# Expert-key stage: another order of VectorE's work in a tile

## What is computed

```python
q = jnp.einsum('btd,ed->bte', hidden_states, W_q)
q = q.reshape(b, t, 2, h, n).transpose(2, 0, 1, 3, 4)
sim = jnp.einsum('pbthn,hkpn->pbthk', q, keys)              # 4 heads, 2 sides, 64 keys
scores_xy, idx_xy = jax.lax.top_k(sim, K)                   # the 8 best of each side
all_scores = (sx[..., :, None] + sy[..., None, :]).reshape(b, t, h, K * K)
scores, pk = jax.lax.top_k(all_scores, K)                   # the 8 best pairs
w = jax.nn.silu(jnp.einsum('btd,bthkd->bthk', hidden_states, de) * jax.nn.softmax(scores, axis=-1))
experts_states = jnp.einsum('bthk,bthkd->btd', w, ue)
dense = jnp.einsum('bti,di->btd', jax.nn.silu(jnp.einsum('btd,id->bti', hidden_states, W_up)), W_down)
return dense + experts_states
```

## Time and profile before

| | |
|---|---|
| three runs | median 1125.65 us (1123.56 to 1127.57) |
| profiled execution | 1118.98 us, its span 1116.8 us |
| PE busy | 994.8 us (89% of the span) |
| DVE busy | 799.0 us (72%) |
| ACT busy | 652.5 us (58%) |
| POOL busy | 497.9 us (45%) |
| mean granted TensorE clock | 0.963 of full speed |

### The profile page before, as it was taken

The page is one execution under the profiler, slowest core; times in us unless marked ns, Lnnn a source line. Parts: engine busy times, 40 slices in busy tenths (PEclk is TensorE's granted clock), DMA queues, the critical chain, the costliest instruction groups (busy, mean ns, idle before and its releaser), DMA issues.

```text
span 1116.8 us, 17009 instructions
## 1 busy us (share of the span) xinstructions
PE 994.8 (89%) x5550; PEld 632.4 (57%) x5550; DVE 799.0 (72%) x1755; ACT 652.5 (58%) x874; POOL 497.9 (45%) x550
## 2 busy tenths in 40 slices
PE   8889999989778989989999788899998887999991
PEld 3345344434457878778877563344443333888881
DVE  7767688887889798798987446788888844444443
ACT  4357667666566866777777524576675650455550
POOL 6558897896415435335434422215061634222220
PEclk9899999999999999999999989999999988999996
DMA  7855979648999500000003231465644247222226
GB/s 247 239 167 159 291 206 346 196 153 270 235 224 221 117 1 1 0 2 1 1 29 79 75 65 57 123 209 142 172 133 129 83 149 284 61 69 74 70 59 225
DMA packets 74200, 149.87 MB, mean 134 GB/s; under 512 B 7823, under 2 KB 44577, under 8 KB 72580
## 3 DMA queue, kind: packets, MB, share of 16 engines
q1 hardware_dynamic: 61380, 98.80, 33.8%
q0 software_dynamic: 10800, 47.63, 12.0%
q10 hardware_dynamic: 1936, 2.36, 0.6%
HBM read 73.14 MB, written 76.25 MB: 134 GB/s over the span
## 4 chain that ended last, share of the span: by engine, by line
PE 63%; DVE 16%; ACT 9%; issue 4%; POOL 4%; DMA 3%; SPq 1%; ACTq 0%; DVEq 0%; POOLq 0%
PE ps L1318 16%; PE ps L1452 10%; PE ps L1433 7%; PE ps L1418 5%; PE ps L1392 4%; PE ps L1402 4%; PE ps L1660 3%; PE ps L1637 3%; ACT pt L1105 3%; PE ps L1623 3%; DVE negmax L1859 2%; PE ps L1461 2%; PE ps L1783 1%; DVE moe_w L2205 1%; PE ps L1336 1%
## 5 line engine op out<-in xcount | busy, mean ns | idle before, releaser
L1859 DVE TENSOR_REDUCE negmax<-ps 128x2 f32<-128x1024 f32 x256 | 309.6, 1222 | 56.6 <-PE ps L1418 54.1
L1105 ACT ACTIVATE pt<-ps 128x1024 f32<-128x1024 f32 x256 | 259.2, 1027 | 136.1 <-PE ps L1433 134.5
L1452 PE MATMUL ps<-pt,v_aug 128*32 128x512 f32 x1024 | 143.1, 621 | 4.5 <-POOL pt L804 3.6
L1433 PE MATMUL ps<-sq,sk 57*128 57x512 f32 (+1 forms) x512 | 127.5, 496 | 6.0 <-DMA sq<-m_sb 3.5
L1418 PE MATMUL ps<-sk,sq 56*128 56x512 f32 (+1 forms) x512 | 107.8, 424 | 21.2 <-ACT pt L1105 16.1
L804 POOL TENSOR_TENSOR pt<-pt,near 128x256 f32<-128x256 f32 x128 | 92.4, 730 | 49.1 <-ACT pt L1105 48.4
L1433 PEld LDWEIGHTS ps<-sq,sk 57*128 57x128 f32 (+1 forms) x512 | 48.5, 186 | 105.7 <-issue 70.7
L996 POOL DMA_INDIRECT expert_out<-yo,dest x39 | 38.1, 976 | 117.4 <-ACT yo L1285 102.6
L908 POOL TENSOR_TENSOR w_first<-w_first,moe_w 128x1024 f32<-128x1024 f32 x16 | 38.1, 2383 | 106.4 <-DVE pt L2197 105.7
L1623 PE MATMUL ps<-sel,hl 128*128 128x512 f32 x256 | 73.4, 422 | 13.3 <-DVE pt L2197 13.3
L1418 PEld LDWEIGHTS ps<-sk,sq 56*128 56x128 f32 (+1 forms) x512 | 49.4, 190 | 42.4 <-ACT pt L1105 27.9
(11 more groups left out here) (323 smaller groups left out, 2083.6 us busy)
## 6 DMA issues: line engine op xcount, KB each, us to landing
expert_rows<-zero SPq DMA_DIRECT2D x3, 5586.0 KB, 61.4
expert_weights_split<-wst POOLq DMA_DIRECT2D x8, 2048.0 KB, 8.7
qk_rows<-hl SPq DMA_DIRECT2D x30, 512.0 KB, 3.1
sk<-qk_rows SPq DMA_DIRECT2D x62, 192.0 KB, 5.1
sq<-qk_rows SPq DMA_DIRECT2D x62, 192.0 KB, 4.5
moe_w<-in_w POOLq DMA_DIRECT2D x16, 512.0 KB, 7.7
wexp<-expert_weights_split POOLq DMA_DIRECT2D x16, 512.0 KB, 4.9
wexp<-expert_weights_split SPq DMA_DIRECT2D x4, 2048.0 KB, 16.4
```

The source lines that it names most:

```text
L1105: act.activation(pt[:, 4 * (U % 2) + 2 * half:4 * (U % 2) + 2 * half + 2, :], ps[:, bank:bank + 2, :], ACT.Exp, scale=(BIAS, SCALE)[L]).th ...
L1433: ins = pe.matmul(ps[:, key.bank + s, :], sk[r, pair, c * P:(c + 1) * P], sq[r, pair, :], start=True, stop=True)
L1452: ins = pe.matmul(ps[32 * j:32 * j + 32, OBANK, :], v_aug[:, b % 2, c, HG * g + j, :], pt[:, 4 * (U % 2) + j, :], start=(c == 0), stop=(c ...
L1859: dve.tensor_reduce(negmax[:, n % 2, col:col + 9:8], ps[:, job.bank:job.bank + 2, :], AX, ALU.max, negate=True).then_inc(s_jd, 1)
```

## The change

Only the order of VectorE's stream changes; no instruction is added or removed on any engine. `top8(n)` is cut into `side_top8(n)` (with the wait for `s_cl` at its head) and `pair_top8(n)`. In the loop, `side_top8(s + 1)` moves ahead of `turned_low(s)`; `norm1` moves from the middle of odd steps to the step before, ahead of `mask(s, 0)` (and stays in step 1, ahead of its first mask); `norms8(s)` moves behind `times_hidden(s, 3)`; `pair_rest` moves from the middle of an odd step to the end of the even step ahead of it (in step 15 the last one stays where it was).

```diff
--- before.py
+++ after.py
@@ -1999,6 +1999,10 @@
                     dve.tensor_scalar(xnb_first[p][:, t % 2, :], x_tok[:, 0, t, :], mv1[:, t, 0:1], rstd1[:, t:t + 1], ALU.subtract, ALU.mult).then_inc(s_n1, 1)
 
             def top8(n):
+                side_top8(n)
+                pair_top8(n)
+
+            def side_top8(n):
                 r = n % RING
                 if n >= 2:
                     dve.wait_ge(s_cl, n - 1)
@@ -2011,6 +2015,10 @@
                 own(dve.tensor_tensor(s64[:, n % 2], sxy[:, r, :, 0, :].unsqueeze(3).broadcast_to([P, RH, 8, 8]),
                                       sxy[:, r, :, 1, :].unsqueeze(2).broadcast_to([P, RH, 8, 8]), ALU.add))
                 own(dve.tensor_reduce(mag[:], sxy[:, r].rearrange("p h s j -> p h (s j)"), AX, ALU.add, apply_absolute_value=True))
+
+            def pair_top8(n):
+                r = n % RING
+                sim = simcat[n % 2].rearrange("p (h s k) -> p h s k", h=RH, s=2)
                 for h in range(RH):
                     own(dve.max_index(ix8[:, h, :], sxy[:, r, h, 0, :], sim[:, h, 1]))
                 own.wait()
@@ -2262,9 +2270,10 @@
                     dve.tensor_scalar(xnb[:, t % 2, :], x_tok[:, 0, t, :], mv[:, 0, t, 0:1], rstd[:, 0, t:t + 1], ALU.subtract, ALU.mult).then_inc(s_cn, 1)
 
             for s in range(NTL):
+                if 2 <= s + 1 < NTL:
+                    side_top8(s + 1)
                 if s >= 2:
                     turned_low(s)
-                odd_norm = s % 2 and (s + 3) // 2 < NTL // 2
                 if s % 2 and s >= 5:
                     pair_sum((s - 5) // 2)
                 if s == 3:
@@ -2275,7 +2284,9 @@
                 if s in (10, 13):
                     rstd2_seed(s // 13, s // 13 + 1)
                 if 2 <= s + 1 < NTL:
-                    top8(s + 1)
+                    pair_top8(s + 1)
+                if s == 1 or s >= 2 and s % 2 == 0 and s // 2 + 2 < NTL // 2:
+                    norm1(2 + s // 2)
                 if s == 15:
                     dve.wait_ge(s_r2, 1)
                     first_cx(0)
@@ -2283,12 +2294,9 @@
                     mask(s, 0)
                     mask(s, 1)
                     times_hidden(s, 0)
-                    if odd_norm:
-                        norm1((s + 3) // 2)
                     mask(s, 2)
                     times_hidden(s, 1)
-                    norms8(s)
-                    if s % 2 and s >= 5:
+                    if s == 15:
                         pair_rest((s - 5) // 2)
                     mask(s, 3)
                     times_hidden(s, 2)
@@ -2300,6 +2308,9 @@
                     first_cx(1)
                 if s:
                     times_hidden(s, 3)
+                    norms8(s)
+                if s % 2 == 0 and s >= 6:
+                    pair_rest((s - 6) // 2)
             row_low("q", 0)
             row_low("q", 1)
             pair_sum(NTL // 2 - 2)
```

## The result

The changed kernel took 1115.04 us (median of 4 runs, 1110.39 to 1117.99), the kernel before on the same chip 1126.61 (1123.56 to 1129.07): ratio 0.989, 95% interval 0.985 to 0.993. The forecast was 1113.9 against 1125.65, a ratio of 0.9896. Timed once more on another chip, the two had 1124.03 and 1129.85, ratio 0.9924 (0.9887 to 0.9962). The kernel is faster, by 0.4 to 1.5%.

The account below looks back on a forecast made before the run. PE was taken as nearly the bound, losing time in stops. Tiles 4 to 13 -12.2, tile 14 +1.2, tile 15 -1.3, tiles 1 to 3 +0.6, together -11.7: from 1125.65 to 1113.9 us, range 1107 to 1125.

Parts of the forecast that it names:

- What bounds the tile: Tiles 4 to 13: PE nearly the bound; odd tiles lose 1.51 at the first mask and 2.56 at their end.
- a third loss, the clock: PE after an odd tile's stops: part of the next tile ran at 1.2 GHz, hidden(10) taking 1.56 more.
- Odd tile, 20.4 forecast: Odd tiles: 19.25 without the two losses, plus 1.14 for late logits(s, 2), gives 20.4; both waits at the end go.
- Even tile, 20.13 forecast: Even tiles: new wait for GpSimd's pairs at the head makes logits(s, 2) 1.23 late, 18.90 becoming 20.13.
- as ScalarE is: Odd tile's head: DVE ready for the first mask 6.4 after the tile's hidden start, the same time as ScalarE.
- Tile 14: Tile 14, even and so far without a stop, was to become 1.2 longer.
- Tiles up to 3: Tiles 1 to 3: masks' saved 2.0 against 2.4 of norms and wait; +0.6, between -2 and +2.
- Tile 15: PE's wait of 1.34 for a norm standing behind norms8 was to go: -1.3.
- VectorE stays the bound: Rival: odd tiles' last product comes later, so even tiles take 21.6 instead of 20.1; 1122.7 us, chance 0.12.
- The clock falls: Rival: two PE stops per tile bring half speed, 18.7 over twelve tiles, 1132.6 us; decides from eight tiles; chance 0.12.
- No change: Rival: the new wait lengthens even tiles to 22.2, as much as odd ones gain; 1125 us, chance 0.13.
- More: Rival: ScalarE's expand comes 1.1 earlier, remaining stops go too, 12 x 1.15 more; 1100 us, chance 0.07.

Follow-up runs that it names:

- e5: Changed kernel with a third buffer for the sums of pairs, so side_top8 waits for clamped pairs one tile earlier; tiles 4-13 204.62 us, ratio to before 0.9893.
- e3: Kernel before with only the layer norms moved ahead of even tiles' first mask; tiles 4-13 218.18 us, ratio 1.0056.
- e10: Kernel before with only the head norms moved to each tile's end; tiles 4-13 208.76 us, ratio 0.994.
- e4: Kernel before with only head norms at the tile's end and the pair sums' rest at even tiles' end; tiles 4-13 206.91 us, ratio 0.9919.
- e11: Changed kernel with the layer norms back in the middle of odd tiles; tiles 4-13 204.48 us, ratio to before 0.9889.
- e1: Changed kernel without the split, the whole choice of keys behind turned_low; tiles 4-13 210.75 us, ratio to before 0.9987.
- e8: Kernel before with layer norms ahead of even tiles' first mask and head norms at each tile's end; tiles 4-13 211.30 us, ratio 0.9974.
- e6: Changed kernel with ScalarE's clamped_silu moved ahead of ff_silu; tiles 4-13 203.82 us, ratio to before 0.9833.
- e7: Changed kernel with both a third pair-sum buffer and ScalarE's clamped_silu ahead of ff_silu; tiles 4-13 203.65 us, ratio to before 0.9851.
- e2: Kernel before with only the choice of keys split in two, the first part ahead of turned_low; tiles 4-13 213.67 us, ratio 0.998.
- e9: Changed kernel with third pair-sum buffer, early clamped_silu and, in odd tiles, weight_silu(s - 1, 3) ahead of x_high; tiles 4-13 201.64 us, ratio to before 0.985.

## Why the prediction was right, by its own steps

**What bounds the tile.** Right: the two waits of the earlier trace rows at an odd tile's end went. The stop ahead of `logits(s, 2)` shrank from 1.51 to 1.11 (forecast 1.14). What I called a third loss, the clock, went too: all ten tiles ran at 1.00, and the sum had this in it, since it was made from 18.90 and not from the 20.5 of tiles 8 and 10; 3.2 of the 12.2 rest on this.

**Odd tile, 20.4 forecast.** Measured 20.33 to 20.36, and 21.98 in tile 13, which has the key projection (21.7). The turned low half ended at H + 3.1 (forecast 3.2), `logits(s, 2)` started at H + 7.72 (7.75), `x_low` at 488.04, H + 17.2 (17.2).

**Even tile, 20.13 forecast.** Measured 20.25 in three, 20.16 in tile 4 and 20.41 in tile 10. DVE went on at H + 0.89 (1.05). The mask came at H + 6.72 instead of 6.5 and `logits(s, 2)` at H + 8.06 instead of 7.84. The 0.12 too little have two sources. The terms as I listed them (1.05, 1.61, 0.6, 2.6, 0.73) add up to H + 6.59, and I wrote 6.5. And VectorE was ready at H + 6.50 (the norm of 456.39 ends at 457.13), though the norm began after a gap of 0.23 that I had not counted; the mask came 0.22 later because it waited for ScalarE's exponential (457.35, above). e5 then showed that the wait for GpSimd, on which the working of the even head rests, is not what sets the even tile, for without it the mask waits for ScalarE and the tile stays at 20.25. I had taken ScalarE's time from an odd tile (H + 5.23) and wrote "as ScalarE is"; in even tiles the exponential is at H + 5.57, behind `x_high`. Two limits lay side by side, and I named the wrong one with nearly the right number.

**The three parts.** The sum treated the parts as one, and that was its luck: priced alone, I gave the norm's move 5 to 7 (e3), and it lost 2.0. One order of adding them, in tiles 4 to 13:

| Kernel | Tiles 4-13 | Step |
|---|---|---|
| before | 216.15 | |
| + head norms at the tile's end (e10) | 208.76 | -7.4 |
| + pair sums at the even tile's end (e4) | 206.91 | -1.9 |
| + choice in two parts (e11) | 204.48 | -2.4 |
| + norm ahead of the even mask (after) | 204.66 | +0.2 |

Of the first step 3.2 are the two even tiles that no longer run at the lower clock. Alone, against before, the split gives 2.5 and the norm's move loses 2.0 (1.6 of it one more tile at the lower clock). Without the split the norm's move costs 3.8 in company of the head norms and pair sums (e1 against e4; 2.3 of it in tile 10 with its clock of 0.93) and 2.5 beside the head norms alone (e8 against e10), as even tiles grow from 20.25 to 20.75 and from 19.8 to 20.56; with it, nothing. What 2.83 against 0.74 seemed to promise never came: half of it lies in the wait for the third exponential, and the other half moves to the next instruction that meets a head sum.

**Tile 14.** +1.2, as forecast.

**Tiles up to 3.** +1.6 instead of +0.6, inside the -2 to +2. e5 shows that without the new wait for GpSimd tiles 2 and 3 are 1.7 shorter: here the wait is on the path. 0.9 of the +1.6 lies in tiles 0 and 1, at a lower clock (0.96 against 1.00, 0.84 against 0.90); tile 0 took 14.58 in before, e5, e6 and e7 and 15.21 in the changed kernel, with the same order in it.

**Tile 15.** PE's wait of 1.34 for the norm went, and from the start of `hidden(15)` to the instruction that had waited it is 20.68 instead of 21.97. But the total from tile 15 on stayed the same. Behind a wait of some 3.4 for ScalarE that both kernels have, the clock was lower in the changed one. The same stretch of the program, first after, then before:

```profile
634.00:644.00 10.00, 9.65 (x34) 7.62 (x35) 0.78 (x2) 1.92 (x3) 5.60 (x3) 0.68 0.80 171
```

```profile
643.00:653.00 10.00, 9.88 (x42) 7.99 (x43) 2.31 (x3) 2.29 (x4) 5.38 (x3) 0.83 0.74 160
```

The other runs settle what this term was worth. e11 has the same code here as the changed kernel and comes to that wait of 3.4 at the same place (H + 39.66 and 39.64), but took 60.08 from tile 15 on, at a clock of 0.97, as before's 61.71 had; the changed kernel's 61.72 are at 0.94. e4 took 60.29 at 0.97. So at the same clock the 1.3 is there (1.4 to 1.6), and the changed kernel's execution lost it again to the clock. Its second execution did so too (61.77), and so did e2's, without the gain (62.96). What decides between the two is open.

**The rivals.** "VectorE stays the bound" needed even tiles of 21.6, which are 20.25. "The clock falls" needed eight tiles at half speed, and none of 4 to 14 has any, with stops of 0.2 to 0.7 us twice in nearly every tile. In e1, with stops of up to 1.6, one tile of ten had 0.93. What the Trainium skill, "TensorE: Matmul & The Clock Gate", section "A second HAM failure mode: psum-queue depth-cycling", tells of one kernel, a TensorE that idled briefly but often and swung between the two clocks, did not happen here: the row of tiles 4 to 13 shows 1.00. "No change" needed even tiles of 22.2. "More" needed ScalarE's exponential 1.1 earlier; e9 brought 0.8 of that in even tiles with another order of ScalarE's queue, and with the third buffer -3.0 in tiles 4 to 13.

**The total.** -11.6 by the first medians, -5.8 by the second, -8.7 by the stage. The forecast of 11.7 is 3 above the stage's own figure: +0.7 from tiles 4 to 13, all of it in even tiles, +1.0 from the first tiles, +1.3 from tile 15. That the first median met it to the us is chance.

## What to carry to other kernels

Where an instruction waits in a shared resource for another engine's long instruction, removing it can move the wait to the next one that needs the resource, as in e3 and e8, as long as that engine has long instructions left to run: count those, and look for other waits that the removed time had covered, before counting the busy time of the one that shows it. Test the parts of a change together and alone, since here a part that lost 2.0 alone cost nothing in company, and the reason was the slack that another part made. Before shortening the engine that PE waits for, look whether a second one is late by almost as much, and whether it is busy without a gap from a wait for PE: then only work put ahead of that wait helps.

## What the runs showed of the hardware

- Some instructions of VectorE wait, inside their own duration, for GpSimd's running head sum of 2.38: two norms of 128x256 took 2.81 to 2.83 beside one and 0.72 to 0.74 without, the 128x32 product 1.43 to 1.73 and 0.18, the two pair sums 2.15, 1.70 (beside the clamped pairs) and 0.86. The masks, which read `ps` in PSUM, took 1.25 to 1.28 throughout. The Trainium skill, "SBUF — State Buffer", section "Who interferes with whom", says that a VectorE instruction with two inputs in SBUF contends with a GpSimd instruction that reads SBUF, and that one with at most one such input, outside the two-port modes, does not; product, pair sums and masks agree. It counts `tensor_scalar`, the norm's operation, among those that can enter these modes. That removing one such wait left the distance of the masks as it was (e3: 12.2 against 12.3 before, e8 and e10: 10.5 both) I had not expected.
- The same code behind the stage took 450.5 to 462.2 us over the profiled executions (e5's left out), so ±0.5% of the total come and go without any edit, while tiles 4 to 13 of one kernel repeated within 0.2 us (204.66 and 204.82).
